# Attention block with paired maximum products on 32-row tiles, a new turn order, later statistics, earlier gate loads and split bias additions

## What is computed

```python
x = x + tanh(g_xattn[0]) * L0_xattn(layernorm(x), ctx, mask, ...)   # pooling of context rows
x = x + tanh(g_ffn[0])   * L0_ffn(layernorm(x), ...)                # FFN, weights merged from 8 experts per batch
x = x + tanh(g_xattn[1]) * L1_xattn(layernorm(x), ctx, ...)         # attention
x = x + tanh(g_ffn[1])   * L1_ffn(layernorm(x), ...)                # 16 columns, top 1, layer norm
```

```python
attn = einsum('bhnd,bhmd->bhnm', q * scale, k)
attn = softmax(attn, axis=-1)
out = einsum('bhnm,bhmd->bhnd', attn, v)
return out @ w_proj.T + b_proj
```

## Time and profile before

| | us |
|---|---|
| runs | 1489.57, 1489.88, 1501.89 |
| median | 1489.88 |
| profiled execution | 1487.68 |
| its span, first to last instruction | 1485.9 |
| busy in the span: PE, DVE, ACT, POOL | 1357.3, 1018.4, 617.1, 544.0 |
| PE banks L1234 (maximum products) | 197.5, 512 of them |

### The profile page before, as it was taken

How to read it: one execution, slowest core, us unless ns; L and a number is a source line. 1 busy time by engine, 2 the same in 40 slices (tenths; PEclk the granted TensorE clock), 3 DMA queues, 4 the chain that set the end, 5 groups by cost and what they waited for, 6 DMA issues and landing times. The chain is left out here.

```text
span 1485.9 us, 32750 instructions
## 1 busy us (share of the span) xinstructions
PE 1357.3 (91%) x12672; PEld 963.2 (65%) x12672; DVE 1018.4 (69%) x1961; ACT 617.1 (42%) x1370; POOL 544.0 (37%) x829
## 2 busy tenths in 40 slices
PE   3687999999999984899999999989999698999997
PEld 3464677777777762577776777766777583655555
DVE  6777665676567765788887888877888535544544
ACT  4434212211221122666666666655666543123221
POOL 0676888788860004233222232322331154000000
PEclk9999999999999996899999999999999789999998
DMA  8205445454531007677666677766772000000000
GB/s 243 69 1 173 134 136 164 121 162 130 159 112 64 32 1 98 128 101 93 88 85 85 86 98 97 92 74 83 98 92 34 1 1 1 13 13 12 25 12 25
DMA packets 92775, 120.26 MB, mean 81 GB/s; under 512 B 7414, under 2 KB 78899, under 8 KB 90348
## 3 DMA queue, kind: packets, MB, share of 16 engines
q1 hardware_dynamic: 83436, 87.82, 35.2%
q0 software_dynamic: 9216, 30.73, 7.5%
HBM read 96.42 MB, written 22.10 MB: 80 GB/s over the span
## 5 line engine op out<-in xcount | busy, mean ns | idle before, releaser
L1123 DVE TENSOR_REDUCE s_neg_max<-banks 112x1 bf16<-112x487 f32 x512 | 323.9, 663 | 87.6 <-PE banks L1234 84.7
L1059 ACT ACTIVATE s_prob<-banks 128x448 f32<-128x448 f32 x512 | 265.9, 547 | 177.2 <-PE banks L1256 176.9
L640 DVE TENSOR_TENSOR s_m<-banks,s_base 128x512 f32<-128x512 f32 x256 | 164.7, 686 | 128.8 <-PE banks L794 128.6
L1234 PE MATMUL banks<-s_k_t,s_q_t 96*112 96x487 bf16 x512 | 197.5, 387 | 1.8 <-DVE s_neg_max L1123 1.8
L1256 PEld LDWEIGHTS banks<-s_q_t,s_k_t 112*128 112x128 bf16 x2048 | 143.0, 99 | 81.1 <-issue 32.7
L1256 PE MATMUL banks<-s_q_t,s_k_t 112*128 112x112 bf16 x2048 | 186.9, 214 | 2.9 <-issue 2.2
L794 PE MATMUL banks<-s_gate_sel,s_tw 64*128 64x256 f32 x1024 | 146.7, 406 | 0.9 <-DVE s_m L640 0.8
L834 PE MATMUL banks<-s_m,s_act_t 128*112 128x256 f32 x512 | 129.8, 389 | 5.9 <-DVE x_res L659 5.9
L1270 PE MATMUL banks<-s_prob,s_v 128*32 128x112 f32 (+1 forms) x4096 | 127.5, 263 | 8.2 <-issue 8.1
L817 PEld LDWEIGHTS banks<-s_x_t,s_m 128*128 128x128 f32 x1024 | 119.1, 191 | 21.4 <-issue 20.9
L817 PE MATMUL banks<-s_x_t,s_m 128*128 128x112 f32 x1024 | 130.5, 280 | 0.1
(11 more groups left out here) (263 smaller groups left out, 2177.2 us busy)
## 6 DMA issues: line engine op xcount, KB each, us to landing
k_parts<-s_k_split POOLq DMA_DIRECT2D x64, 281.2 KB, 3.7
s_k_t<-k_parts SPq DMA_DIRECT2D x32, 562.5 KB, 7.9
s_tw<-in_tw SPq DMA_DIRECT2D x16, 1024.0 KB, 5.1
s_k_raw<-in_ctx_k POOLq DMA_DIRECT2D x64, 187.5 KB, 3.8
s_k_t<-k_parts SPq DMA_DIRECT2D x32, 375.0 KB, 9.9
s_v_raw<-in_ctx SPq DMA_DIRECT2D x32, 256.0 KB
s_src<-in_ctx SPq DMA_DIRECT2D x8, 896.0 KB, 14.5
s_k_t<-k_parts SPq DMA_DIRECT2D x32, 187.5 KB, 11.1
```

The source lines that it names most:

```text
L640: nc.vector.tensor_tensor(dst[:, :, :, rows_], got, base[:, :, rows_].unsqueeze(2).broadcast_to([P, 2, B, HR]), ALU.add).then_inc(S["merge ...
L1059: nc.scalar.activation(prob[t % 2][:, c, :], w.bank(SCORE + n % SRING, P, TILE), ACT.Exp, scale=DH ** -0.5).then_inc(S["exp_done"], 1)
L1123: nc.vector.tensor_reduce(neg_max[half][:, ROWS + h, 0:1], w.bank(MAX + n % MRING, T, NKEY), AX.X, ALU.max, negate=True).then_inc(S["max_d ...
L1234: nc.tensor.matmul(w.bank(MAX + n % MRING, T, NKEY), q_t[k][0:ROWS, h, :], k_t[k][0:ROWS, h, FIRST:FIRST + NKEY], start=True, stop=True).t ...
```

## The change

- The maximum product of a head is now made over 32 rows (slots 0 and 1: first part of the query by first and second part of the key), and two heads are computed as a pair, the even one on rows 0 to 31, the odd one on rows 32 to 63 (`q_odd`, to which ScalarE copies the odd heads' 32 query rows in `odd_queries`). The slots of the parts are renumbered so that these two come first; all six still enter the scores. The rest of the product is left out of the maximum alone, which is only subtracted before the exponential.
- Three banks hold the pairs (`MAX_BANKS`), the third also the transposed maxima; `MAX_FREE` says how many maxima must have been read before a pair.
- The turn tables of all four engines are written in another order.
- Statistics for stage 3: 8 batches in stage 2's last chunk, one after every second pair; the other 24 in three groups of 8 between VectorE's first steps of stage 3. `rstd` is computed in two parts.
- POOL, not ScalarE and VectorE, writes the heads' rows of buffers 1 and 2.
- The nine inputs of the gates are loaded at the end of stage 1's list on SP.
- ScalarE loads the square root's table at the end of stages 2 and 3.
- In stage 4 POOL adds `ln_b` to the first 16 batches ahead of the `kept` additions, and VectorE normalises batches 4 to 7 ahead of the sums of squares.

```diff
+                for name, dst in w.gate.items():
+                    sp.dma_start(dst[:], a[name]).then_inc(w.gate_in, 16)
...
-                for dst, name in pairs:
-                    sp.dma_start(dst[:], a[name]).then_inc(loads, 16)
...
-                        if p:
-                            pair_statistics(p - 1)
-                    pair_statistics(PAIRS - 1)
-
-                def pair_statistics(p):
-
-                    dve.wait_ge(S["x_done"], nth(PAIRS * (FC - 1) + p))
-                    for b in (2 * p, 2 * p + 1):
-                        last = nc.vector.bn_stats(stats[:, b, :], w.x_res[:, b, :])
-                    chain.link(last)
-                    for b in (2 * p, 2 * p + 1):
-                        last = nc.vector.bn_aggr(w.mean_var[:, b, :], stats[:, b, :])
+                        if p % 2:
+                            early_statistics(p // 2)
+
+                def early_statistics(b):
+
+                    dve.wait_ge(S["x_done"], nth(PAIRS * (FC - 1) + b // 2))
+                    chain.link(nc.vector.bn_stats(stats[:, b, :], w.x_res[:, b, :]))
+                    nc.vector.bn_aggr(w.mean_var[:, b, :], stats[:, b, :])
...
+                nc.scalar.activation(w.table[:], w.ident[:, 0:1], ACT.Sqrt)
...
-    SCORE, MAX, NEG, OUT, PREP, TAIL = 0, 2, 4, 5, 6, 7
-    RING, SRING, MRING = 3, 2, 2
+    SCORE, MAX, OUT, PREP, TAIL = 0, 2, 5, 6, 7
+    RING, SRING = 3, 2
+    MAX_BANKS = ((0, 1), (0, 1), (2, 0), (1, 2), (0, 1), (0, 1), (2, 0), (1, 2))
+    MAX_FREE = (-1, 2, 3, 5, 7, 10, 11, 13)
...
-                    for row, n in ((0, 3), (3, 2), (5, 1)):
+                    for row, n in ((0, 2), (2, 3), (5, 1)):
...
+                    if b < 2:
+                        place_heads(b + 1)
+
+                def place_heads(k):
+
+                    wait(pool, "q_parts_done", k)
+                    nc.gpsimd.tensor_copy(k_t[k][ROWS:ROWS_MAX, :, FIRST:FIRST + S2],
+                                          w.ident[ROWS:ROWS_MAX, ROWS:ROWS_MAX].unsqueeze(2).broadcast_to([H, H, S2]))\
+                        .then_inc(rows_ready[k], 1)
+                    pool.wait_ge(rows_ready[k], 2)
...
+                    at(b + 3, key_parts)
+                    at(b + 2, put_values)
                     at(b + 1, bias)
-                    at(b + 2, second_parts)
-                    at(b + 2, key_parts)
-                    at(b + 2, query_parts)
-                    at(b + 3, put_values)
+                    at(b + 3, query_parts)
+                    at(b + 4, second_parts)
...
+                def odd_queries(b):
+                    wait(act, "q_t_done", 2 * b + 2)
+                    wait(act, "max_ps", H // 2 * (b - 1))
+                    nc.scalar.activation(q_odd[b % 2][SLOT:2 * SLOT, :, :], q_t[b % RING][0:SLOT, 1:H:2, :],
+                                         ACT.Copy).then_inc(S["q_odd_done"], 1)
...
+                variances(0, EARLY)
+                inverses(0, EARLY, 1)
...
+                        late_statistics(2 * EARLY, 3 * EARLY)
...
+                    if (b, n) == (0, 0):
+                        late_statistics(3 * EARLY, B)
+                        variances(EARLY, B)
+                    if (b, n) == (1, 1):
+                        inverses(EARLY, B, 2)
...
-                def scores_by_query(b, h):
-                    k, n = b % RING, H * b + h
-                    if h == 0:
+                def scores_by_query(b, pair):
+                    k = b % RING
+                    if pair == 0:
                         wait(pe, "k_t_done", 2 * b + 2)
                         wait(pe, "q_t_done", 2 * b + 2)
+                        wait(pe, "q_odd_done", b + 1)
                         pe.wait_ge(k_in[k], 48 * (b // RING + 1))
-                    wait(pe, "max_done", n - MRING + 1)
-                    nc.tensor.matmul(w.bank(MAX + n % MRING, T, NKEY), q_t[k][0:ROWS, h, :],
-                                     k_t[k][0:ROWS, h, FIRST:FIRST + NKEY], start=True, stop=True).then_inc(S["max_ps"], 1)
+                    wait(pe, "max_done", H * b + MAX_FREE[pair])
+                    if pair == 2:
+                        wait(pe, "neg_done", 2 * b)
+                    if pair == 6:
+                        wait(pe, "neg_done", 2 * b + 1)
+                    nc.tensor.matmul(w.bank(MAX + MAX_BANKS[pair][0], T, NKEY), q_t[k][0:SLOT, 2 * pair, :],
+                                     k_t[k][0:SLOT, 2 * pair, FIRST:FIRST + NKEY], start=True, stop=True)
+                    nc.tensor.matmul(w.bank(MAX + MAX_BANKS[pair][1], T, NKEY), q_odd[b % 2][SLOT:2 * SLOT, pair, :],
+                                     k_t[k][SLOT:2 * SLOT, 2 * pair + 1, FIRST:FIRST + NKEY],
+                                     start=True, stop=True).then_inc(S["max_ps"], 1)
...
+                def add_ln(first, end):
+                    for b in range(first, end):
+                        wait(pool, "xn_done", b + 1)
+                        nc.gpsimd.tensor_tensor(w.x_res[:, b, :], w.x_res[:, b, :], ln_b[:], ALU.add).then_inc(S["x_biased"], 1)
+
+                wait(pool, "biased", 1)
+                add_ln(0, B // 2)
                 for b in range(B):
                     wait(pool, "x_tr", b + 1)
                     nc.gpsimd.tensor_tensor(xn[:, b, :], xn[:, b, :], proj_b[:], ALU.add).then_inc(S["kept"], 1)
-                wait(pool, "biased", 1)
-                for b in range(B):
-                    if b == B // 2:
-                        wait(pool, "wts_done", 1)
-                    wait(pool, "xn_done", b + 1)
-                    nc.gpsimd.tensor_tensor(w.x_res[:, b, :], w.x_res[:, b, :], ln_b[:], ALU.add).then_inc(S["x_biased"], 1)
+                wait(pool, "wts_done", 1)
+                add_ln(B // 2, B)
...
+                norm(1)
                 chain.link(nc.vector.tensor_tensor(sumsq[:], w.rstd[:, :, 0], w.rstd[:, :, 0], ALU.mult))
                 chain.link(nc.vector.tensor_tensor(sumsq[:], sumsq[:], w.mean_var[:, :, 1], ALU.mult))
                 nc.vector.tensor_scalar(sumsq[:], sumsq[:], float(D), 1e-24, ALU.mult, ALU.max).then_inc(S["radicand_done"], 1)
-                norm(1)
```

219 lines of the change are left out of this document (115 added, 104 removed).

## The result

The changed kernel takes 1442.69 us (median of four runs, 1440.29 to 1445.82) where the kernel before took 1490.32 beside it: a ratio of 0.966 between the means of the runs, 95% interval 0.961 to 0.972 (0.968 between the medians). Of the 47.4 us between the two profiled spans (1485.9 and 1438.5), each place of the program has its share.

The account below looks back on a forecast made before the run. TensorE was taken to bound the stage 3 loop, with waits at four places outside it. +6.8 - 8.5 - 1.3 - 1.0 - 2.7 - 6.2 = -12.9 us gave 1474.8 for the profiled execution, 1477 as median; range 1443 to 1506.

Parts of the forecast that it names:

- undisturbed turns: Stage 3 loop: one batch's attention without gaps, 16.89 us, set by TensorE; VectorE 2.2 us to spare, ScalarE 5.5.
- 16.89 + 0.22 = 17.1: Stage 3 turn: eight pair visits at 0.45 us replace two products of 0.41, one change shared; +6.8 us over 31 turns.
- Cheap visits: Rival, stage 3: switching TensorE to a pair's arrangement and back costs nothing, visit 0.21 us, turn near 16.1; 1445; chance 0.22.
- Dear visits: Rival, stage 3: a pair's second tile waits for the first's weights or stream, visit 0.60 us; 1514 us; chance 0.17.
- End of stage 2: Last chunk: one batch's statistics per two pairs of batches, 2.1 us for two pairs instead of 1.57 each; -8.5 us.
- Start of stage 2: Gate inputs loaded in stage 1, so TensorE's first hidden product waits only for normalising; -1.3 us (0 to -2.1).
- Fill: Start of stage 3: shorter preamble's 2.6 us lost to late statistics, head rows off ScalarE -2.4, POOL +1.4; net -1 us.
- Stage 4 from the logits on: POOL's first 16 additions come earlier: logit addition 0.7 us instead of 4.93 (-4.2), clock holds (-2.0); together -6.2 us.
- Start of stage 4: Table load off the chain, -1.1 us; POOL's and small VectorE additions out of the way, -1.6 us; together -2.7.

Follow-up runs that it names:

- keys in two: Kernel before, second and third key transfers of a batch held about half a turn behind the first: 1473.89 us against 1489.39 (0.988).
- the version without the copy: New kernel with two single 96-row maximum products in place of each pair, and without ScalarE's copy of the odd heads' queries: 1436.85 us.

## Why the prediction was wrong, and where it was right

**The step that failed** is one sentence on what bounds the kernel: "What the loop takes beyond its undisturbed turns is gaps of TensorE that the profile calls issue; nothing in the change aims at them and I leave them as they are." That was 19 us I had seen and booked as a constant: 28 turns of before take 17.57 us on average, of the new kernel 16.89 (17.4 us by the loop without key transfers). The change has a part that bears on them. "The slots of the parts are renumbered" reads as bookkeeping, but it changes which rows the key transfers go to. That shortens the burst behind which TensorE's instructions wait (11.8 to 9.6 us, medians), and from 10.2 down few gaps are left. Shown from both sides: new rows in the old kernel, 551.75 to 539.57 us; old rows in the new kernel, 533.38 to 541.52; and three other ways of making the burst shorter, broken or longer (no keys, keys in two, an extra transfer) moved the gaps as this cause asks. Every gap ends 1.2 to 1.7 us after an instruction packet.

**A second term was missing in the turn.** "16.89 + 0.22 = 17.1" had the pairs right: with single products the new turn is 16.66 and with pairs 16.89, +0.23. What it lacked is that the new order by itself takes 0.23 us off, 16.89 to 16.66, so that the two cancel. In an old turn the starts next to maximum products are 0.01 to 0.05 us late (0.226 on average where 0.21 is reached, 0.056 for 0.05), too little for the profile to call them waits. Why is not shown. I had looked only for orders that lose. 31 x 0.23 = 7 us, and 17 to 19 of gaps: 24 to 26 us, where the loop was missed by 25.

**Cheap visits, the first rival, came near the time by another way.** It gave 1445, but through a visit of 0.21 us and a turn of 16.1. The visit is 0.43 and the turn 16.88. The time alone would have confirmed a wrong mechanism. Dear visits (0.60) are out too, since the second tile starts within 0.01 us of the first.

**End of stage 2**: -8.5 forecast, -9.2 between the profiles, -11.1 + 1.6 by undoing it alone. The cadence, 2.05 us for two pairs, is the forecast's 2.1. **Start of stage 2**: -1.3 and -1.5, a match within a scatter of 3 to 4 us. **Fill**: -1.0 and -3.0; I had let late statistics cost the whole of the 2.6 us that the shorter preamble wins, and undoing them alone gives 1.6, which the scatter of the fill covers. **Stage 4 from the logits on**: -6.2 and -6.7, with the mechanism as told (0.69 for 4.93, 6.28 for 9.19).

**Start of stage 4**: -2.7 forecast, -8.7 between the profiles, and most of the excess is not the change's. The stretch from the first gate product to the first column product has the same TensorE work in all versions: 45.77 in the kernel before, but 39.51 in its copy without key transfers and 44.12 with new rows; 39.35 in the new kernel, but 45.36 with old rows and 47.91 in the version without the copy. The granted clock goes with it: 0.80, 0.91, 0.82, 0.92, 0.79 and 0.74. What sets it I did not find; it is no gain of the edits. The share that is, from the last exponential to the first gate product, was 16.96 to 14.71, with 16.34 when only POOL's additions go back: -2.3 for -2.7 forecast.

**The chances.** Faster by over 1% had 0.44, and it was. The range ended at 1443 because I had let it end just below the cheap visits' 1445; the gaps had no bounds in it at all, neither 0 nor 19, though the trace showed them and an unexplained 19 us is an unknown of that size. With 0 to 19 us for them it would have begun near 1425.
